# Seven block products in place of eight in the second inner layer of passes 13 to 15, with block sums on GpSimd

## The chip, the cores and the metric

One NeuronCore of one Trainium2 chip. The metric is the device time of one launch in microseconds (us). The kernel before takes 1303.97 us (median of three runs, 1303.16 to 1304.44).

## The reference, cut to what matters

For x of shape 4 x 1024 tokens x 256 features:

```python
x = x + 0.5 * ffn(layernorm(x))        # first feed-forward
x = x + attn(layernorm(x))             # a long convolution, gelu, 256 x 256 projection
x = x + 0.5 * ffn(layernorm(x))        # second feed-forward, same weights

def ffn(x):                            # einsum('bsi,oi->bso') * a scale per output
    h = silu(lin(x, w1, s1)) * lin(x, w2, s2)   # 256 -> 1024
    h = gelu(lin(h, h1, s_h1))                  # 1024 -> 1024, first inner layer
    h = gelu(lin(h, h2, s_h2))                  # 1024 -> 1024, second inner layer
    return lin(h, w3, s3)                       # 1024 -> 256
```

All weights of the feed-forward are -1, 0 or 1; the scales are float32. The result is float32.

## The kernel before, in words

**Passes.** The 4096 tokens are eight chunks of 512. A pass takes one chunk through one feed-forward, so there are 16 passes: 0 to 7 the first feed-forward, 8 to 15 the second. The convolution of batch b runs in eight units beside passes 4 to 13. Passes 13, 14 and 15 have almost only the feed-forward left; in the first slots of pass 13 the last batch is projected (`projection`, L1492) and added (`residual`, L889).

**Precision.** Each activation tile (128 features x 512 tokens) is kept as two float16 tiles, a high part and a low part, and every weight tile is multiplied by both into the same float32 sum in PSUM. The weights are exact in float16. One inner layer is 8 output tiles x 8 input tiles x 2 parts = 128 matmuls of 128 x 512.

**What each engine does in an inner layer.** For output tile s TensorE adds up its 16 products in a PSUM bank (`hidden`, L1413). ScalarE applies gelu in the bank (`gelu`, L1176) and makes the high part (`split_high`, L1166); VectorE makes the low part (`split_low`, L641) and with it a sum into `los`, from which the end of the program learns whether all numbers were finite. The next layer needs both parts of all eight tiles. So that TensorE need not wait for the last of them, it begins a layer with its first three output tiles side by side: their products with input tiles 0 to 5, then 6, then 7 (`EARLY`).

**Slots.** The order on every engine is written out in the program; nothing is chosen on the chip. A pass has 26 slots: 0 to 7 first inner layer, 8 to 15 second, 16 to 25 the mixed part, where TensorE makes the up projections of the next pass and the two down groups of this one. `T(i, s)` is slot s of pass i. In each slot an engine does its part of the layer and then what `fixed` (VectorE, L907) or `slot` (ScalarE, TensorE) puts there: for the next pass the statistics (`sums`, L676), from them the scales on GpSimd (`scales_of`, L1028), the normalised input (`norm`, L1186) and its low part (`norm_low`, L703). These stand in slots that `norm_slots` gives: in pass 13 `sums` and `scales_of` in slot 5, `norm` in 7 and 11, `norm_low` in 8 and 12; in pass 14 `sums` and `scales_of` in slot 2, `norm` in 4 and 7, `norm_low` in 5 and 8. In pass 15 there is no next pass.

**Queues are in order.** An instruction that waits holds up all that stands behind it on its engine. In `fixed`, `same` comes ahead of `sums`.

**PSUM.** Five banks (psf) go round for the feed-forward, three (pss) serve the convolution and the projection. Projection pairs 0 and 3 both use bank pss0, so pair 3 waits for the residual of pair 0.

**The check of the weights.** `same` (L710) compares a float16 weight piece with the float32 original, which SyncE loads again (`load_again`, L1604): 11 pieces of 2048 columns, in passes 13 to 15.

**The end.** Behind the last inner layer come the down products of pass 15 in three groups; VectorE multiplies and adds each (`down`, L661), checks the sums, and SyncE stores the rows.

## Time and profile before

| | |
|---|---|
| median of three runs | 1303.97 us |
| the profiled execution's own time | 1306.01 us |
| its span, first to last instruction | 1304.2 us |
| TensorE (PE) busy | 1293.1 us, 99% of the span |
| VectorE (DVE) busy | 888.8 us, 68% |
| ScalarE (ACT) busy | 762.9 us, 58% |
| GpSimd (POOL) busy | 402.6 us, 31% |
| mean granted TensorE clock | 0.999 of 2.4 GHz |

The profiled execution takes 1.81 us more than its span, and 2.04 us more than the median of the runs. A line such as "L1421 PE MATMUL psf<-hab,wall" is a group of instructions of one line of the program: engine, operation, destination and sources by their names. "x" is a count.

### The profile page before, as it was taken

Reading aid. Unit: us, or ns where it says so; the run is one execution under the profiler, and the core shown is the slowest. Engines: PE = TensorE matmul, PEld = TensorE weight load, DVE = VectorE, ACT = ScalarE, POOL = GpSimd, SP = SyncE. Lnnn points to the kernel's source line nnn. Section 1 sums busy time; section 2 is a strip of 40 time slices with the busy share of each in tenths; the row PEclk is TensorE's granted clock in tenths of the full one; section 3 lists DMA queues with packets and bytes.
Section 4 is the critical chain, followed back from the end, with each engine's and each line's share of the span. In section 5 each row is a group of like instructions: output and inputs, shape, how many; then the busy total and the mean of one; then the engine's idle time right before and its main releaser. Section 6 shows DMA issues by size and latency. Waiting matters only on the chain.

```text
span 1304.2 us, 17940 instructions
## 1 busy us (share of the span) xinstructions
PE 1293.1 (99%) x7039; PEld 653.2 (50%) x7039; DVE 888.8 (68%) x1768; ACT 762.9 (58%) x1245; POOL 402.6 (31%) x396
## 2 busy tenths in 40 slices
PE   9999999999999999999999999999999999999998
PEld 3454454644545445455454554545545455454544
DVE  5287768432546987988779887898877974454723
ACT  4664556845457467574775747757467564545433
POOL 6821377700012422633226333262332600001000
PEclk9999999999999999999999999999999999999999
DMA  8310000000010000000000000000000002221300
GB/s 314 136 41 9 9 1 17 1 9 9 1 53 13 2 15 1 17 1 1 17 1 17 9 9 17 17 12 14 9 17 17 9 17 74 81 81 56 138 1 19
DMA packets 45469, 41.80 MB, mean 32 GB/s; under 512 B 32704, under 2 KB 42432, under 8 KB 42688
## 3 DMA queue, kind: packets, MB, share of 16 engines
q1 hardware_dynamic: 45232, 40.56, 10.2%
q8 instruction: 57, 0.93, 0.3%
q14 instruction: 36, 0.29, 0.1%
q10 hardware_dynamic: 144, 0.02, 0.0%
HBM read 28.51 MB, written 4.19 MB: 25 GB/s over the span
## 4 chain that ended last, share of the span: by engine, by line
PE 93%; DVE 5%; issue 1%; ACT 1%; POOL 0%; POOLq 0%; DVEq 0%
PE psf L1421 66%; PE psf L1409 15%; PE psf L1433 7%; PE pss L1498 2%; DVE hab L645 1%; PE pss L1478 1%; DVE arena L602 1%; PE pss L1488 1%; PE pss L1449 1%; DVE xr L886 1%; DVE xr L674 0%; DVE psf L668 0%; DVE arena L605 0%; PE pss L1463 0%; DVE ht L657 0%
## 5 line engine op out<-in xcount | busy, mean ns | idle before, releaser
L1421 PE MATMUL psf<-hab,wall 128*128 128x512 f16 x4096 | 890.7, 379 | 2.8 <-DVE xr L674 1.8
L1421 PEld LDWEIGHTS psf<-hab,wall 128*128 128x128 f16 x4096 | 400.1, 98 | 482.4 <-DVE xr L674 3.2
L1180 ACT ACTIVATE psf<-psf,scf 128x512 f32<-128x512 f32 x256 | 168.7, 659 | 383.5 <-PE psf L1421 382.7
L645 DVE SCALAR_TENSOR_TENSOR hab<-psf,hab 128x512 f16<-128x512 f32 x256 | 174.9, 687 | 278.6 <-ACT hab L1173 277.7
L1409 PE MATMUL psf<-h,wall 128*128 128x512 f16 x1024 | 234.8, 381 | 1.0 <-ACT h L1184 0.7
L1173 ACT ACTIVATE hab<-psf 128x512 f16<-128x512 f32 x256 | 152.8, 597 | 8.1
L1409 PEld LDWEIGHTS psf<-h,wall 128*128 128x128 f16 x1024 | 99.8, 98 | 115.1 <-issue 2.5
L657 DVE SCALAR_TENSOR_TENSOR ht<-psf,scf,sil 128x512 f32<-128x512 f32 x128 | 93.9, 748 | 85.7 <-PE psf L1409 44.0
L1032 POOL TENSOR_SCALAR rs<-mv 128x4 f32<-128x4 f32 x16 | 5.3, 334 | 456.0 <-DVE mv L688 456.0
L1163 ACT ACTIVATE sil<-psf,scf 128x512 f32<-128x512 f32 x128 | 86.2, 685 | 83.0 <-PE psf L1409 82.2
L1433 PE MATMUL psf<-wall,hab 128*128 128x256 f16 x1024 | 117.1, 273 | 0.3
L1433 PEld LDWEIGHTS psf<-wall,hab 128*128 128x128 f16 x1024 | 99.3, 98 | 17.2 <-DVE xr L674 1.8
L645 DVE SCALAR_TENSOR_TENSOR hab<-ht,hab 128x512 f16<-128x512 f32 x128 | 105.8, 834 | 2.5
L834 DVE TENSOR_TENSOR arena<-arena,g 128x896 f32<-128x896 f32 (+6 forms) x112 | 103.4, 927 | 2.1
L1173 ACT ACTIVATE hab<-ht 128x512 f16<-128x512 f32 x128 | 80.2, 627 | 28.2 <-DVE ht L657 27.7
L837 DVE TENSOR_TENSOR arena<-arena 128x896 f32<-128x896 f32 (+6 forms) x112 | 96.2, 859 | 0.3
L1084 POOL TENSOR_TENSOR arena<-arena 128x1024 f32<-128x1024 f32 x8 | 23.2, 2895 | 235.8 <-ACT arena L1271 235.8
L1095 POOL TENSOR_TENSOR arena<-arena,g 128x896 f32<-128x896 f32 (+6 forms) x56 | 85.6, 1528 | 27.1 <-DVE hab L645 23.6
L1099 POOL TENSOR_TENSOR arena<-arena 128x896 f32<-128x896 f32 (+6 forms) x56 | 89.8, 1603 | 4.2
L1193 ACT ACTIVATE xnp<-xr,rn,rs 128x128 f32<-128x128 f32 x120 | 49.1, 481 | 3.5 <-POOL rn L1040 3.2
L1163 ACT ACT_TABLE_LOAD x31 | 39.8, 1283 | 0.5
L602 POOL TENSOR_TENSOR g16b<-arena 128x16 f32<-128x16 f32 (+5 forms) x72 | 35.7, 517 | 2.8
(143 smaller groups left out, 917.4 us busy)
## 6 DMA issues: line engine op xcount, KB each, us to landing
arena<-wh SPq DMA_DIRECT2D x8, 1024.0 KB, 5.4
g<-wh SPq DMA_DIRECT2D x6, 1024.0 KB, 9.2
out<-xr SPq DMA_DIRECT2D x15, 256.0 KB, 2.2
xr<-x SPq DMA_DIRECT2D x7, 512.0 KB, 5.0
arena<-w SPq DMA_DIRECT2D x3, 1024.0 KB, 5.1
g<-w SPq DMA_DIRECT2D x2, 1024.0 KB, 6.6
xr<-wh SPq DMA_DIRECT2D x2, 1024.0 KB, 9.5
g<-w SPq DMA_DIRECT2D x2, 512.0 KB, 6.0
```

Of the source, the lines that this page charges most:

```text
L645: e.scalar_tensor_tensor(out=hab[:, buffer(p), m, 1, :], in0=source(p), scalar=2.0 ** E2 if l else 1.0, in1=hab[:, buffer(p), m, 0, :], op ...
L657: e.scalar_tensor_tensor(out=source(p), in0=psf[bank_use(i, "up", 2 * m + 1) % MAIN][:, :], scalar=scf[:, 1, m:m + 1], in1=sil[:, m % 2, : ...
L834: muls[j] = ch.done(e.tensor_tensor(tv, xf[:, c, 0:NB - j], gj, ALU.mult))
L837: total = free[ti] = ch.done(e.tensor_tensor(acc[:, c, j:NB], acc[:, c, j:NB], tv, ALU.add))
L1095: k = ch.done(e.tensor_tensor(tv, xf[:, 0, 0:NB - j], g3[:, 0, j, ds].unsqueeze(1).to_broadcast([P, NB - j, P]), ALU.mult))
L1099: add = e.tensor_tensor(acc[:, 0, j:NB], acc[:, 0, j:NB], tv, ALU.add)
L1163: e.activation(sil[:, m % 2, :], psf[bank_use(i, "up", 2 * m) % MAIN][:, :], ACT.Silu, scale=scf[:, 0, m:m + 1]).then_inc(s_silu, 1)
L1173: e.activation(hab[:, buffer(p), m, 0, :], source(p), ACT.Copy, scale=2.0 ** E2 if l else 1.0).then_inc(s_hi, 1)
L1180: e.activation(bank, bank, ACT.Gelu, scale=scf[:, 2 + l, m:m + 1]).then_inc(s_gelu, 1)
L1409: ins = e.matmul(bank[:, :], W12[:, m // 4, l, k, ms], h0[:, k, part, :], start=(k == 0 and part == 0), stop=(k == 1 and part == 1))
L1421: ins = e.matmul(bank[:, :], WH[:, l, m // 2, k, ms], hab[:, buffer(p), k, part, :], start=(k == 0 and part == 0), stop=(k == KH - 1 and p ...
L1433: ins = e.matmul(bank[:, half:half + D], hab[:, buffer(p), k, part, P * t:P * (t + 1)], W3[:, k, :], start=(k == 0 and part == 0), stop=(k ...
```

## The change

The second inner layer of passes 13, 14 and 15 is computed as a 2 x 2 block product with seven block products. Weights are cut into four blocks of 512 x 512 (A11, A12, A21, A22), activations into four of 512 features x 256 tokens. For each of the seven products one weight block (or a sum of blocks) is multiplied with one activation block (or a sum of blocks), and the results are added to the four output blocks. A product is 4 output tiles x 4 input tiles x 2 parts = 32 matmuls of 128 x 256.

- **Sums of weight blocks.** Four (`sum_weights`), on VectorE, once: in slot 15 of pass 12 and in slots 0, 2 and 4 of pass 13. They are float16.
- **Sums of activation blocks.** The output tiles of the first inner layer come in the order 0, 4, 1, 5, 2, 6, 3, 7; two that follow each other are a quad q (tiles q and q+4, four blocks of 128 x 256). Gelu goes to SBUF (`gelu_words`). `turn_tokens` makes the sums T1 and T3 (one operation of 512 columns), T2 and T4 (256 each). GpSimd does it for quads 0, 1 and 2, in its slots 1, 3 and 4 and behind what stands there already; VectorE for quad 3. Then the high and low parts of seven blocks are made: for quads 0 to 2 one operation of 1792 columns on ScalarE (`high_quad`) and one on VectorE (`low_quad`), for quad 3 in parts of 768, 512 and 512 columns.
- **Products.** A PSUM tile holds two products, left and right half, and there are 14 tiles per layer. The first seven tiles take their left halves for input tiles 0, 1, 2 and then 3 side by side. All eight banks go round in passes 13 to 15 (`fast_uses`), each reused for the eighth use after it.
- **Output sums.** VectorE adds the halves (`first_sums`, `middle_sums`, `last_sums`: 512, 512 + 256 and 512 columns per quad), ScalarE copies one tile in two quads (`keep`), applies gelu in SBUF (twice 512) and makes the high parts, VectorE the low parts.
- **The last down products** of pass 15 take rows 0, 4, 1, 5, then 2, 6, then 3, 7, for three token tiles side by side ahead of the last two rows.
- **Checks.** `same` moves to other slots (T(13, 6), (13, 20), (13, 23), (14, 2), (14, 4), (14, 20), (14, 23), (15, 0), (15, 2), (15, 4), (15, 6)), works in place, and its pieces are loaded into xr rows once the output of these has been stored. `check_ternary` in pass 3 tests w*w*w = w for the second inner layer's weights: eight times two float16 products and one comparison of 1024 columns.

```diff
-SAME_AT = [T(13, s) for s in (9, 10, 14, 25)] + [T(14, s) for s in (2, 3, 10, 11, 12, 25)] + [T(15, 3)]
-
-AGAIN = {13: ((0, 1), (2, 3, 4, 5)), 14: ((), (6, 7, 8, 9, 10))}
+SAME_AT = [T(13, s) for s in (6, 20, 23)] + [T(14, s) for s in (2, 4, 20, 23)] + [T(15, s) for s in (0, 2, 4, 6)]
+AGAIN = {13: ((0, 1), (2, 3)), 14: ((4,), (5, 6, 7, 8)), 15: ((), (9, 10))}
+TERNARY = range(6, 10)
+CUBES_BESIDE = [2000] * 16 + [700] * 4 + [1400, 700, 700, 1400, 700, 700]
...
+FAST = 13
+QD, HF = KH // 2, CH // 2
+ROWS = [m + QD * r for m in range(QD) for r in range(2)]
+G12, G11, G22, G21, T1, T3, T2, T4 = range(8)
+U1, U3, U2 = T1, T3, T2
+WIDE = 7 * HF
+OPERAND = {1: G11, 2: G21, 3: G22, 4: T4, 5: T1, 6: T2, 7: T3}
+T_PARTS = ((G11, T1), (T1, T2), (T2, T4 + 1))
...
+SUMS_OF_WEIGHTS_AT = {T(12, 15): 0, T(13, 0): 1, T(13, 2): 2, T(13, 4): 3}
+def parts(l, q):
+    if l == 2:
+        return ((0, 2), (2, 4)) if q + 1 == QD else ((0, 4),)
+    return T_PARTS if q + 1 == QD else ((G11, T4 + 1),)
...
+def tiles_of(i):
+    return [t for q in (0, 2) for t in [("keep", i, q)] + [(kind, i, q + n) for n in range(2)
+                                                           for kind in ("first", "middle", "last")]]
...
+        def released(use):
+            kind, i, n = use
+            if kind == "h":
+                return s_gelu, gelus(i, n)
+            if kind == "u":
+                return (s_gate if n % 2 else s_silu), KH * i + n // 2 + 1
+            if kind == "d":
+                return s_xup, 2 * i + n + 1
+            n = quad(i, n) + 1
+            return {"keep": (s_kept, (n + 1) // 2), "first": (s_u1, n), "middle": (s_c22, n), "last": (s_c1221, n)}[kind]
...
+        def turned(i, q, n):
+            if q + 1 == QD:
+                return s_tokens, 3 * (i - FAST) + n
+            return s_tokensp, 3 * ((QD - 1) * (i - FAST) + q) + n
+        def turn_tokens(e, w, i, q):
+            g, sem = words[q % 2], turned(i, q, 0)[0]
+            w.wait_ge(s_gelu, gelus(i, 2 * q + 1))
+            e.tensor_tensor(both(at(g, T1, 2)), both(at(g, G11, 2)), spread2(at(g, G12)), ALU.subtract).then_inc(sem, 1)
+            w.wait_ge(*turned(i, q, 1))
+            e.tensor_tensor(at(g, T2), at(g, T3), at(g, G11), ALU.add).then_inc(sem, 1)
+            w.wait_ge(*turned(i, q, 2))
+            e.tensor_tensor(at(g, T4), at(g, G21), at(g, T2), ALU.subtract).then_inc(sem, 1)
...
+            def low_quad(i, l, q):
+                for n in range(len(parts(l, q))):
+                    k = split_of(i, l, q, n)
+                    high, low_, of = halves_to(i, l, q, n)
+                    w.wait_ge(s_hiq, k)
+                    c = N_FFN_SPLITS - N_QUAD_SPLITS + k - 1
+                    e.scalar_tensor_tensor(out=low_, in0=of, scalar=2.0 ** E2, in1=high, op0=ALU.mult, op1=ALU.subtract,
+                                           accum_out=los[:, c:c + 1]).then_inc(s_loq, 1)
...
+            def first_sums(i, q):
+                n, g = quad(i, q), words[q % 2]
+                w.wait_ge(s_tile["first"], n + 1)
+                w.wait_ge(s_kept, n // 2 + 1)
+                w.wait_ge(s_loq, words_free(i, 2, q))
+                e.tensor_tensor(two(g, G11, U1 - G11), both(fast_tile("first", i, q)[:, :]),
+                                spread2(at(kept[n // 2 % 2], n % 2)), ALU.add).then_inc(s_u1, 1)
+            def middle_sums(i, q):
+                n, g = quad(i, q), words[q % 2]
+                bank = fast_tile("middle", i, q)
+                w.wait_ge(s_tile["middle"], n + 1)
+                w.wait_ge(s_u1, n + 1)
+                e.tensor_tensor(both(at(g, U3, 2)), both(bank[:, :]), spread2(at(g, U1)), ALU.add).then_inc(s_u23, 1)
+                w.wait_ge(s_u23, n + 1)
+                e.tensor_tensor(at(g, G22), at(bank, 0), at(g, U2), ALU.add).then_inc(s_c22, 1)
+            def last_sums(i, q):
+                n, g = quad(i, q), words[q % 2]
+                w.wait_ge(s_tile["last"], n + 1)
+                w.wait_ge(s_u23, n + 1)
+                e.tensor_tensor(two(g, G12, G21 - G12), both(fast_tile("last", i, q)[:, :]), both(at(g, U3, 2)),
+                                ALU.add).then_inc(s_c1221, 1)
...
+            def sum_weights(which):
+                a11, a12, a21, a22 = (WH[:, 1, 2 * r:2 * r + 2, QD * c:QD * (c + 1), :] for r in range(2) for c in range(2))
+                s1, s2, s3, s4 = (t[:, :, :, :] for t in sums16)
+                if which == 0:
...
+            def fast_layers(i):
+                for s in range(KH):
+                    if s % 2:
+                        if s == 7:
+                            turn_tokens(e, w, i, 3)
+                        low_quad(i, 1, s // 2)
+                    slot(i, s)
+                slot(i, 8)
+                slot(i, 9)
+                first_sums(i, 0)
+                middle_sums(i, 0)
+                slot(i, 10)
+                last_sums(i, 0)
+                slot(i, 11)
+                first_sums(i, 1)
+                middle_sums(i, 1)
+                last_sums(i, 1)
+                slot(i, 12)
+                low_quad(i, 2, 0)
+                first_sums(i, 2)
+                middle_sums(i, 2)
+                slot(i, 13)
...
+                if t in SUMS_OF_WEIGHTS_AT:
+                    time += sum_weights(SUMS_OF_WEIGHTS_AT[t])
...
+                    if i >= FAST and s in (1, 3, 4):
+                        turn_tokens(e, w, i, (1, 3, 4).index(s))
...
+            def keep(i, q):
+                n = quad(i, q) // 2
+                w.wait_ge(s_tile["keep"], n + 1)
+                if n > 1:
+                    w.wait_ge(s_u1, 2 * n - 2)
+                e.activation(kept[n % 2], fast_tile("keep", i, q)[:, :], ACT.Copy).then_inc(s_kept, 1)
+            def gelu_quad(i, q):
+                n, g = quad(i, q), words[q % 2]
+                upper, lower = (scf[:, 3, r:r + 1] for r in (q, q + QD))
+                w.wait_ge(s_u1, n + 1)
+                w.wait_ge(s_c1221, n + 1)
+                e.activation(at(g, G12, 2), at(g, G12, 2), ACT.Gelu, scale=upper).then_inc(s_gup, 1)
+                w.wait_ge(s_c22, n + 1)
+                e.activation(at(g, G22, 2), at(g, G22, 2), ACT.Gelu, scale=lower).then_inc(s_glow, 1)
+            def high_quad(i, l, q):
+                for n, (lo, hi) in enumerate(parts(l, q)):
+                    high, _, of = halves_to(i, l, q, n)
+                    if l == 1:
+                        w.wait_ge(s_gelu, gelus(i, 2 * q + 1))
+                        if hi > T1:
+                            w.wait_ge(*turned(i, q, 1 if hi <= T2 else 3))
+                    else:
+                        w.wait_ge(s_gup, quad(i, q) + 1)
+                        w.wait_ge(s_glow, quad(i, q) + 1)
+                    e.activation(high, of, ACT.Copy, scale=2.0 ** E2).then_inc(s_hiq, 1)
...
+            def fast_layers(i):
+                for s in range(KH):
+                    gelu_words(i, s)
+                    if s % 2:
+                        high_quad(i, 1, s // 2)
+                    slot(i, s)
+                slot(i, 8)
+                slot(i, 9)
+                keep(i, 0)
+                slot(i, 10)
+                gelu_quad(i, 0)
+                slot(i, 11)
+                gelu_quad(i, 1)
+                high_quad(i, 2, 0)
+                slot(i, 12)
+                keep(i, 2)
+                high_quad(i, 2, 1)
+                slot(i, 13)
+                gelu_quad(i, 2)
+                high_quad(i, 2, 2)
+                slot(i, 14)
+                slot(i, 15)
+                gelu_quad(i, 3)
...
+            def product(i, q, p, out, ks):
+                g = OPERAND[p]
+                ms = slice(P * (q % 2), P * (q % 2 + 1))
+                if p in (3, 5, 6, 7):
+                    w.wait_ge(s_wsum, 4)
+                for k in ks:
+                    w.wait_ge(s_loq, split_of(i, 1, k, PART_OF[g] if len(parts(1, k)) == 3 else None))
+                    if p in (1, 2, 4):
+                        stationary = WH[:, 1, q // 2 + 2 * (p == 4), k + QD * (p != 1), ms]
+                    else:
+                        stationary = sums16[{5: 0, 6: 1, 7: 2, 3: 3}[p]][:, q // 2, k, ms]
+                    for part in range(2):
+                        a = WIDE * part + HF * (g - G11)
+                        ins = e.matmul(out, stationary, regions[k][:, a:a + HF], start=(k == 0 and part == 0),
+                                       stop=(k + 1 == QD and part == 1))
+                return ins
...
+                tiles = tiles_of(i)
+                early, banks = tiles[:7], []
+                for k in range(QD - 1):
+                    for n, use in enumerate(early):
+                        if not k:
+                            banks.append(fast_bank(*use))
+                        left(use, banks[n], (k,))
+                    slot(i, KH + k)
+                for kinds in (("keep", "first", "last"), ("middle",)):
+                    for n, use in enumerate(early):
+                        if use[0] in kinds:
+                            left(use, banks[n], (QD - 1,))
+                for n, use in enumerate(tiles):
+                    if n >= len(early):
+                        banks.append(fast_bank(*use))
+                        left(use, banks[n], range(QD))
+                    right(use, banks[n])
...
-            for t in (0, 2):
-                down(i, t, banks[t // 2], 0, range(KH - 1), False)
+            banks = [fast_bank("d", i, g) for g in range(len(groups(i)))]
+            for rows in (ROWS[:4], ROWS[4:6]):
+                for t in (0, 2, 3):
+                    fast_down(i, t, banks[max(t - 1, 0)], 0, rows, False)
             for g, (t0, n) in enumerate(groups(i)):
                 for t in range(t0, t0 + n):
-                    down(i, t, banks[g], D * (t - t0), (KH - 1,) if t % 2 == 0 else range(KH), t + 1 == t0 + n)
+                    fast_down(i, t, banks[g], D * (t - t0), ROWS if t == 1 else ROWS[6:], t + 1 == t0 + n)
...
-                    w.wait_ge(s_dve, mark["ylo", 2 * B - 1][1])
+                    for c in range(4):
+                        w.wait_ge(s_out[c], 16 * len(groups(NC + c)))
```

## Rows read from the trace of the kernel before

**Rows 1.** The page's first part: busy us, share and instructions of each engine.
```profile
PE 1293.1 (99%) x7039; PEld 653.2 (50%) x7039; DVE 888.8 (68%) x1768; ACT 762.9 (58%) x1245; POOL 402.6 (31%) x396
```

**Rows 2.** Timeline of TensorE, passes 12 to 15: start, length, what, count.
```profile
1061.90 0.86 PE L1488 MATMUL pss<-cs,arena 128*128 128x64 f16 x24
...
1078.92 9.66 PE L1421 MATMUL psf<-hab,wall 128*128 128x512 f16 x44
...
1096.67 0.49 PE L1498 MATMUL pss<-wts,arena 128*128 128x256 f16 x3
...
1160.22 55.42 PE L1421 MATMUL psf<-hab,wall 128*128 128x512 f16 x256
1215.47 7.07 PE L1409 MATMUL psf<-h,wall 128*128 128x512 f16 x32
1222.38 3.66 PE L1433 MATMUL psf<-wall,hab 128*128 128x256 f16 x32
1225.87 3.62 PE L1409 MATMUL psf<-h,wall 128*128 128x512 f16 x16
...
1291.53 5.19 PE L1433 MATMUL psf<-wall,hab 128*128 128x256 f16 x46
```

**Rows 3.** Groups by shape, GpSimd: busy, mean ns of one, idle before.
```profile
L1037 POOL TENSOR_TENSOR rs<-rs,half 128x4 f32<-128x4 f32 x16 | 21.0, 1314 | 1.3
...
L602 POOL TENSOR_TENSOR g16b<-arena 128x512 f32<-128x512 f32 x12 | 13.9, 1179 | 0.5
...
L1099 POOL TENSOR_TENSOR arena<-arena 128x512 f32<-128x512 f32 x8 | 11.3, 1413 | 0.4
...
L602 POOL TENSOR_TENSOR g16b<-arena 128x256 f32<-128x256 f32 x12 | 7.3, 633 | 0.5
```

**Rows 4.** Groups by shape, ScalarE.
```profile
L1180 ACT ACTIVATE psf<-psf,scf 128x512 f32<-128x512 f32 x256 | 168.7, 659 | 383.5 <-PE psf L1421 382.7
...
L1156 ACT ACTIVATE wall<-g 128x2048 f16<-128x2048 f32 x5 | 9.5, 1901 | 0.0
```

**Rows 5.** Groups by shape, VectorE.
```profile
L645 DVE SCALAR_TENSOR_TENSOR hab<-psf,hab 128x512 f16<-128x512 f32 x256 | 174.9, 687 | 278.6 <-ACT hab L1173 277.7
...
L716 DVE SCALAR_TENSOR_TENSOR arena<-arena,wall 128x2048 f16<-128x2048 f32 x11 | 25.2, 2290 | 6.2 <-DMA arena<-wh 6.2
...
L724 DVE SCALAR_TENSOR_TENSOR arena<-arena 128x1024 f16<-128x1024 f32 x16 | 18.9, 1220 | 0.0
```

**Rows 6.** Timeline of VectorE, pass 14: the end of the statistics for pass 15.
```profile
1177.87 0.38 DVE L688 BATCH_NORM_AGGREGATE mv<-st 128x2 f32<-128x6 f32 x4
```

**Rows 7.** Timeline of GpSimd, pass 14: the last two of four scale operations.
```profile
1178.89 3.01 POOL L1037 TENSOR_TENSOR rs<-rs,half 128x4 f32<-128x4 f32 x1
1181.98 0.20 POOL L1040 TENSOR_TENSOR rn<-rn,rs 128x4 f32<-128x4 f32 x1
```

**Rows 8.** Timeline of ScalarE, pass 14: one half of the next pass's input.
```profile
1182.22 1.65 ACT L1193 ACTIVATE xnp<-xr,rn,rs 128x128 f32<-128x128 f32 x4 [3.24 <-POOL rn L1040]
1183.90 0.63 ACT L1197 ACTIVATE xnp<-xnp 128x512 f16<-128x512 f32 x1
```

**Rows 9.** Timeline of VectorE around slot 15 of pass 12.
```profile
1060.01 1.22 DVE L724 SCALAR_TENSOR_TENSOR arena<-arena 128x1024 f16<-128x1024 f32 x1
1061.16 0.08 DVE L724 DVE_READ_ACCUMULATOR arena<-arena 128x1 f32 x1
```

**Rows 10.** Timeline of VectorE, the last down groups, first and last of six.
```profile
1296.75 0.70 DVE L668 TENSOR_TENSOR psf<-psf,s3b 128x512 f32<-128x512 f32 x1 [1.05 <-PE psf L1433]
...
1299.41 0.42 DVE L674 TENSOR_TENSOR xr<-xr,psf 128x256 f32<-128x256 f32 x1
```

**Rows 11.** Stretches of 2 us near the start: busy times, then granted clock (PEclk), DMA.
```profile
8.00:10.00 2.00, 1.33 (x8) 0.62 (x7) 1.59 (x7) 1.31 (x3) 1.24 (x3) 1.00 1.06 435
10.00:12.00 2.00, 1.66 (x5) 0.54 (x5) 0.93 (x2) 0.06 (x2) 0.56 (x2) 0.59 1.01 426
12.00:14.00 2.00, 2.00 (x7) 0.71 (x6) 0.40 (x1) 0.64 (x1) 1.69 (x1) 0.56 1.02 430
```

More of the change, by code:

```diff
@@ L1 @@
+import itertools
 import math
@@ new lines, in halves_to @@
+        def halves_to(i, l, q, part):
+            lo, hi = parts(l, q)[part]
+            if l == 1:
+                a, z = HF * (lo - G11), HF * (hi - G11)
+                return regions[q][:, a:z], regions[q][:, WIDE + a:WIDE + z], at(words[q % 2], lo, hi - lo)
+            if hi - lo == 2:
+                row = q + QD * (lo // 2)
+                return hab[:, i % 2, row, 0, :], hab[:, i % 2, row, 1, :], at(words[q % 2], lo, 2)
+            tiles = hab[:, i % 2, q:q + QD + 1:QD, :, :]
+            return tiles[:, :, 0, :], tiles[:, :, 1, :], both(at(words[q % 2], 0, 4))
@@ L963, in slot @@
                 beside = TAPS_BESIDE if i < FIRST - 1 else PAIRED if paired else BESIDE
-                quota = (0 if s < 0 else beside[s]) - fixed(i, s)
-                strand.run(now["slot"], quota)
+                time = fixed(i, s)
+                strand.run(now["slot"], (0 if s < 0 else beside[s]) - time)
+                cubed.run(now["slot"], CUBES_BESIDE[s] - time)
             e.memset(one[:, :], 1.0).then_inc(s_init, 1)
@@ L1349, in act_program @@
             for i in range(PASSES):
-                for s in range(2 * KH):
-                    gelu(i, s)
-                    split_high(tile(i, 1, s))
-                    slot(i, s)
+                if i >= FAST:
+                    fast_layers(i)
+                else:
+                    for s in range(2 * KH):
+                        gelu(i, s)
+                        split_high(tile(i, 1, s))
+                        slot(i, s)
                 if i + 1 < PASSES:
-                    behind = tile(i + 1, 0, 0)
+                    behind = 0
                     for n, (what, m) in enumerate(MIXED):
@@ L1424, in hidden, with first_hidden @@
                         ins.then_inc(s_hid, 1)
+            def first_hidden(i, s, bank, ks):
+                row = ROWS[s]
+                ms = slice(P * (row % 2), P * (row % 2 + 1))
+                for k in ks:
+                    w.wait_ge(s_lo, tile(i, 0, k) + 1)
+                    for part in range(2):
+                        ins = e.matmul(bank[:, :], WH[:, 0, row // 2, k, ms], hab[:, i % 2, k, part, :],
+                                       start=(k == 0 and part == 0), stop=(k == KH - 1 and part == 1))
+                    if k == KH - 1:
+                        ins.then_inc(s_hid, 1)
@@ new lines, in fast_down @@
+            def fast_down(i, t, bank, half, rows, count):
+                for m in rows:
+                    q, r = m % QD, m // QD
+                    w.wait_ge(s_loq, split_of(i, 2, q, r if q + 1 == QD else None))
+                    for part in range(2):
+                        ins = e.matmul(bank[:, half:half + D], hab[:, i % 2, m, part, P * t:P * (t + 1)], W3[:, m, :],
+                                       start=(m == ROWS[0] and part == 0), stop=(m == ROWS[-1] and part == 1))
+                    if m == ROWS[-1] and count:
+                        ins.then_inc(s_down, 1)
```

234 lines of the change are left out of this document (205 added, 29 removed).

## The prediction

> **What bounds the kernel now.** The page's busy shares come first: TensorE is busy for 99% of the span, VectorE 68%, ScalarE 58% [rows 1]. Then its timeline over the last passes: one piece of work stands directly behind the other, 256 matmuls of both inner layers from 1160.22 to 1215.47 with no gap [rows 2]. So TensorE's instruction stream is the time, and a change pays what it takes out of the stream and costs each place at which TensorE now has to wait. The other engines must be followed in order, since before they always arrive early and after the change they have a longer way to go.
>
> **What goes.** A 512-column matmul takes (1215.47 - 1160.22)/256 = 0.2158 us, a 256-column one with a new weight tile each time (1225.87 - 1222.38)/32 = 0.1091 us [rows 2]. Before: 128 x 0.2158 = 27.63 us a layer. After: 7 x 32 x 0.1091 = 24.43 us. Gain 3.20 us, three times: **-9.6 us** (between -9 and -10).
>
> **Durations for what comes.** GpSimd's float32 sum of 512 columns took 1.18 us where it had little beside it and 1.41 in the convolution, 256 columns 0.63 [rows 3]: `turn_tokens` is 1.18 + 0.63 + 0.63 and two waits on itself of 0.1, at least 2.65; with 1.41 and the small ones longer in proportion 3.1. I take 2.75, nearer to the quiet row since VectorE mostly waits meanwhile. ScalarE: 0.66 for 512 columns, 1.90 for 2048 [rows 4], so 1.69 for 1792 and 0.87 for 768. VectorE: 0.69, 1.22 and 2.29 for 512, 1024 and 2048 columns [rows 5], so 2.0 for 1792 and 0.95 for 768; `turn_tokens` on VectorE 0.69 + 0.42 + 0.42 [rows 5, 10] and waits on itself, 1.65. A semaphore from one engine to the next costs some 0.05, from TensorE 0.2.
>
> **Pass 14, the large one.** Time 0 is the start of its first inner layer. Tiles are done at 9.5, 9.9, 10.4 (three side by side: 44 matmuls to the first), then 13.8, 17.3, 20.7, 24.2 and 27.6.
> - Quad 0: gelus end 11.05, GpSimd 13.85, ScalarE's high parts 15.6, VectorE's low parts 17.6.
> - Slot 2 of VectorE stands behind these low parts: `same` 2.25, ends 19.85, and only then `sums`, 1.8, ends 21.7. Before, `sums` ended at 1178.25 - 1160.22 = 18.0 [rows 2, 6].
> - GpSimd's slot 2 is `scales_of`, and it waits for these sums; quad 1 stands behind it in slot 3, though its gelus end at 17.0. Before, the last of the scale operations ended 3.93 us behind the sums [rows 6, 7]; the long one of them took 3.01 of that against a mean of 1.31 [rows 3], so I take 2.2: 23.9 (up to 25.6). Quad 1 on GpSimd: 26.65.
> - ScalarE has waited for it with quad 1's high parts: 28.4. Behind: gelu 4 29.1, `norm` 1.65 + 0.63 [rows 8] 31.35, gelu 5 32.05. Quad 2: GpSimd 34.9, ScalarE high 36.65, gelu 6 37.35, gelu 7 38.0; VectorE low parts of quad 2 38.65, `norm_low` 39.3, `turn_tokens` of quad 3 40.95, the first low part of quad 3 **41.95**.
> - TensorE would want quad 3 after 42 matmuls of the new layer, at 27.63 + 4.58 = 32.2. On its way there it also needs the banks of tiles 4, 5 and 6, which gelus 4, 5 and 6 free: it waits until 37.4 for the last, has 3.3 us of work, and then waits for quad 3. **+9.75 us** (9.0 to 12.5: the slow scales, +1.7, GpSimd at 1.41, +0.9).
>
> **Pass 13.** (Times of the trace.) `scales_of` is in slot 5, behind the three quads. But VectorE's low parts of quad 0 now stand ahead of residual 0. Tile 1 is done at 1090.2 and gelu at 1091.05; GpSimd 1093.85, ScalarE 1095.6, VectorE 1097.6, residual 0 1098.3. Projection 3, at 1096.67 before [rows 2], needs its bank: **+1.7** (1.4 to 2.2). Then tile 5 at 1106.6, quad 2's low parts at 1114.0 by the same chain (gelu, 2.75, 1.69, 2.0), behind them `sums` 1.8, `same` 2.25, `turn_tokens` 1.65, low part 0.95: 1120.75. TensorE is there at 1113.5 + 4.6 = 1118.1: **+2.65** (2.2 to 3.5).
>
> **Pass 15.** No scales and no norms. Time 0 as above: quad 1 on GpSimd 20.0, ScalarE 21.7, gelus 4 and 5 23.1, quad 2 on GpSimd 26.1, high 27.8, low 29.8, `same` in slot 6 32.1, `turn_tokens` 33.75, low part 34.7, against 32.2: **+2.5** (2.0 to 3.2).
>
> **Weight sums.** The first (2048 columns, float16) stands in slot 15 of pass 12 ahead of `y_low`, whose end at 1061.24 [rows 9] the inverse transform waits for, on TensorE at 1061.90 [rows 2]: cover 0.65. No row shows a float16 sum of two SBUF tensors. At the rate of the nearest row it is 2.29 [rows 5] and the wait 1.65; at twice that rate 1.15 and **+0.5**. I take 0.5, because float16 outputs are packed here and the other three sums are hidden either way (VectorE idles in slots 0, 2 and 4 ahead of each wait). The Trainium skill (VectorE: DVE Perf Modes, Mode 2x_1P) says that a two-tensor operation on packed 16-bit data gives two results a cycle; by it the term is 0.5, by the float32 row 1.65, and no row of before decides it. `check_ternary` is 24 operations, about 21 us, in pass 3, in portions of 2.6 us a slot beside a split of 0.7 in 3.45 us: 0.
>
> **Second layers and mixed parts.** From the first part of quad 3 on TensorE has 182 matmuls, 19.9 us. VectorE has 3.8 us per quad in it, ScalarE 2.3 and a copy; the last quad's high parts come behind the silu table load and silu 0, its low parts about 8.2 us after the layer, TensorE's first down row 3 at 8.2: 0 (to 0.3). `same` in slots 20 and 23 leaves VectorE 6 us behind the start of the next layer, which wants its last tile 9 us in: 0.
>
> **The end.** Before, 46 matmuls after the layer group 0 is done. After, 56 are (three tiles took their first six rows): +1.1; the last low part comes 4.4 us after the layer, TensorE wants row 7 at 4.15: +0.25. The VectorE chain behind, 1296.75 to 1299.83 [rows 10], stays. **+1.35** (1.1 to 1.8).
>
> **The clock.** In the first 10 us TensorE had short waits (1.33 of 2 us busy) and in the next 4 us its granted clock was 0.59 and 0.56, near 1.2 GHz [rows 11]: some 1.7 us lost. In pass 14 it works 0.9 us in the 9 us before 37.4. I expect the same fall there; 1.25 of what it costs lies in front of the wait for quad 3 anyway. **+1.0** (0 to 3.5). The Trainium skill (TensorE: Matmul & The Clock Gate, Part 1) has the two levels as a gate that follows TensorE's activity; by it the fall comes, and the waits of 1.7 to 2.7 us in passes 13 and 15 could bring it too.
>
> **Sum.** -9.6 + 9.75 + 1.7 + 2.65 + 2.5 + 0.5 + 1.35 + 1.0 = +9.85. Span 1304.2 + 9.8 = 1314.0, own time of the profiled execution 1315.8. That execution lies 2.04 above the median of the runs, so the median becomes 1303.97 + 9.8 = **1313.8 us**.
>
> **Rivals.**
> - *The waits are covered (faster).* One mechanism: the low parts of quad 3 are there when TensorE has done its 42 matmuls. It decides from 32.2 us after the first layer's start. Then 9.75, 2.65, 2.5 and the clock go and the sum is -6.0: 1297.9. For it: before, the layer's own work leaves VectorE and ScalarE 2 to 3 us idle in each slot. Against: the order of GpSimd's queue in pass 14, by which the chain reaches 41.95 with every duration at its lowest still beyond 41. If only pass 14 is covered, -0.9: 1303.1, no change. 7% and 6%.
> - *The clock falls widely (slower still).* It is low for 4 us behind each of the three waits: 1.7 us each, and in pass 14 with none absorbed: +5 in place of +1, 1317.8. For it: rows 11. Against: outside pass 14 no wait is longer than 2.7 us. 15%.
> - *Float16 sums and GpSimd at their slow rows.* +1.15, +0.9 and the slow scales +1.7: 1317.5. 9%.
> - *The 256-column products don't run at 0.1091.* If a product costs an eighth more than that, a layer takes 27.6 us again and the gain of 9.6 is gone: 1323.4. Against: 1024 matmuls of this shape at the steady rate. 3%.
> - The forecast as it stands: 60%.
>
> **How the numbers follow.** Its own range is 1310.5 to 1317; with the two slow rivals to 1318, and below to 1307.5 for parts of the chain that are shorter than I read them. What a measurement can tell from no change is 0.2%, 2.6 us. Faster 0.07, same 0.06, slower 0.87.
>
> **What would show it.** In the profile after: 224 matmuls a layer at 0.109; TensorE's longest waits in pass 14, for ScalarE's gelus and then for a VectorE low part, 9 to 10 us in all; GpSimd's first sum of quad 1 of pass 14 behind its scales; in pass 13 a wait of projection 3 for L889's successor. Wrong would be a GpSimd chain of quad 1 that starts at its gelus, or no wait above 3 us in pass 14.

## The result and the profile after

The changed kernel takes **1321.58 us** (median of 4 runs, 1320.70 to 1324.66) against 1303.97 before: ratio 1.0138, 95% interval 1.0125 to 1.0150. Slower was forecast, by 9.8 us; it became 17.6, outside the range. The profiled execution took 1320.70 us, span 1318.9, and its page begins:

```profile
PE 1285.7 (97%) x7327; PEld 681.4 (52%) x7327; DVE 954.3 (72%) x1831; ACT 771.5 (58%) x1236; POOL 436.0 (33%) x423
```

TensorE's share has fallen from 99% to 97% [rows 1]: its work shrank by 7.4 us, the span grew by 14.7. So the time lies in waits (and in matmuls that a slow clock stretched, which count as busy). Its timeline shows where, beside the place in which before stood 256 matmuls without a gap [rows 2] (start, length, what, count, and in brackets the idle time and what ended it; passes 3, 13, 14 and 15):

```profile
288.16 1.50 PE L1925 MATMUL pss<-g,arena 128*128 128x128 f16 x24 [1.38 <-ACT xr L794]
...
314.58 1.14 PE L1939 MATMUL pss<-arena,cs 128*128 128x256 f16 x9 [0.75 <-issue]
...
1079.74 9.66 PE L1817 MATMUL psf<-hab,wall 128*128 128x512 f16 x44
...
1099.34 0.50 PE L1974 MATMUL pss<-wts,arena 128*128 128x256 f16 x3 [1.69 <-DVE xr L1175]
...
1121.88 0.61 PE L1836 MATMUL pss<-arena,wall 128*128 128x256 f16 x4 [2.67 <-DVE arena L831]
...
1162.56 10.52 PE L1817 MATMUL pss<-hab,wall 128*128 128x512 f16 x48
...
1191.45 0.39 PE L1836 MATMUL psf<-arena,wall 128*128 128x256 f16 x2 [0.22 <-ACT arena L1487]
1194.22 0.39 PE L1836 MATMUL psf<-arena,g 128*128 128x256 f16 x2 [2.38 <-ACT arena L1487]
1200.23 0.61 PE L1836 MATMUL psf<-arena,g 128*128 128x256 f16 x2 [5.61 <-ACT g L1487]
...
1224.76 1.89 PE L1793 MATMUL psf<-h,wall 128*128 128x512 f16 x8
...
1245.56 10.52 PE L1817 MATMUL pss<-hab,wall 128*128 128x512 f16 x48
...
1278.89 0.61 PE L1836 MATMUL psf<-arena,g 128*128 128x256 f16 x2 [4.23 <-ACT g L1487]
...
1285.00 0.61 PE L1836 MATMUL pss<-arena,wall 128*128 128x256 f16 x4 [1.35 <-DVE arena L831]
...
1304.88 1.91 PE L1897 MATMUL psf<-wall,hab 128*128 128x256 f16 x16
```

From these starts and those of [rows 2] (before's pass 15 began at 1236.27) the difference comes apart, against the prediction's terms (us; a pass counts from its first inner layer to the next pass's, pass 15 to the end of its second layer):

| stretch | predicted | measured |
|---|---|---|
| pass 3 (`check_ternary`) | 0 | +2.44 |
| from there to pass 13 (drift; first weight sum) | +0.5 | +0.49 |
| pass 13: -3.2 + 1.7 + 2.65 | +1.15 | +1.52 |
| pass 14: -3.2 + 9.75 + clock 1.0 | +7.55 | +6.95 |
| pass 15: -3.2 + 2.5 | -0.7 | **+4.06** |
| the end | +1.35 | +1.35 |
| sum | +9.85 | +16.81 |

The start behind a wait moves by some 0.16 us more than its bracket says: without a wait, the next start lies that much ahead of a row's recorded end.

The two profiles are only 14.70 apart, because that of before had lost 2.11 at its start (its clock of [rows 11]; the profile after shows 1.00 there) and at 215 us. By about as much, 2.04, that execution lay above the median of its runs. The median after lies 0.88 above its own profiled execution: 16.81 + 0.88 = 17.7, against 17.6 between the medians.

### The profile page after: what moved, and what is told of

Read it like the earlier page. It is cut to its first block and busy times, and to the rows that moved or that the text cites. A ratio compares the mean times of both kernels' runs of the same rounds, so it can differ in the third digit from the quotient of the medians.

```text
span 1318.9 us, 18667 instructions
## 1 busy us (share of the span) xinstructions
PE 1285.7 (97%) x7327; PEld 681.4 (52%) x7327; DVE 954.3 (72%) x1831; ACT 771.5 (58%) x1236; POOL 436.0 (33%) x423
## 5 line engine op out<-in xcount | busy, mean ns | idle before, releaser
L1805 PE MATMUL psf<-hab,wall 128*128 128x512 f16 x3328 | 723.8, 379 | 2.1 <-DVE xr L957 1.7
L1805 PEld LDWEIGHTS psf<-hab,wall 128*128 128x128 f16 x3328 | 325.0, 98 | 392.0 <-DVE xr L957 3.2
L1474 ACT ACTIVATE psf<-psf,scf 128x512 f32<-128x512 f32 x208 | 136.9, 658 | 291.6 <-PE psf L1805 290.8
L810 DVE SCALAR_TENSOR_TENSOR hab<-psf,hab 128x512 f16<-128x512 f32 x208 | 141.8, 685 | 166.4 <-ACT hab L1467 165.5
L1793 PE MATMUL psf<-h,wall 128*128 128x512 f16 x976 | 223.2, 379 | 1.0 <-ACT h L1548 0.7
L1467 ACT ACTIVATE hab<-psf 128x512 f16<-128x512 f32 x208 | 124.2, 597 | 6.6
L820 DVE SCALAR_TENSOR_TENSOR hab<-ht,hab 128x512 f16<-128x512 f32 x120 | 98.8, 832 | 2.2
L1909 PE MATMUL psf<-wall,hab 128*128 128x256 f16 x832 | 95.1, 273 | 0.3
L1909 PEld LDWEIGHTS psf<-wall,hab 128*128 128x128 f16 x832 | 80.6, 98 | 13.9 <-DVE xr L957 1.8
L642 POOL TENSOR_TENSOR arena<-arena 128x512 f32<-128x512 f32 x6 | 9.2, 1539 | 178.4 <-ACT arena L1487 178.4
L1817 PE MATMUL psf<-hab,wall 128*128 128x512 f16 x288 | 63.3, 379 | 0.0
```

Source lines behind the costliest of these rows:

```text
L810: e.scalar_tensor_tensor(out=hab[:, buffer(p), m, 1, :], in0=source(p), scalar=2.0 ** E2 if l else 1.0, in1=hab[:, buffer(p), m, 0, :], op ...
L820: e.scalar_tensor_tensor(out=hab[:, i % 2, m, 1, :], in0=ht[:, n % 3, :], scalar=1.0, in1=hab[:, i % 2, m, 0, :], op0=ALU.mult, op1=ALU.su ...
L1467: e.activation(hab[:, buffer(p), m, 0, :], source(p), ACT.Copy, scale=2.0 ** E2 if l else 1.0).then_inc(s_hi, 1)
L1474: e.activation(bank, bank, ACT.Gelu, scale=scf[:, 2 + l, m:m + 1]).then_inc(s_gelu, 1)
L1793: ins = e.matmul(bank[:, :], W12[:, m // 4, l, k, ms], h0[:, k, part, :], start=(k == 0 and part == 0), stop=(k == 1 and part == 1))
L1805: ins = e.matmul(bank[:, :], WH[:, l, m // 2, k, ms], hab[:, buffer(p), k, part, :], start=(k == 0 and part == 0), stop=(k == KH - 1 and p ...
```

## The experiments

**e1, the scale operations behind the three quads of pass 14 too.**

```
-    if i == FIRST - 1 or i > FIRST and (i - FIRST) % 2 == 0:
+    if i == FIRST - 1 or i > FIRST and (i - FIRST) % 2 == 0 or i == 14:
```

> The changed kernel, with the statistics, scales, norms and their low parts of pass 14 in the slots that pass 13 uses (5, 7 and 11, 8 and 12), so that GpSimd's scales stand behind the three quads. Theory (order of GpSimd's queue, and VectorE beside it): quad 1 of pass 14 then starts at its gelus, but now beside VectorE's comparison in slot 2, and quad 2 beside the one in slot 4, so that GpSimd takes some 5.3 us a quad as in pass 15 and not 2.75. Pass 14, from the start of its first inner layer to the end of its second, goes from 62.2 us to about 59, the whole to about 1318.4. Rival (the order alone, GpSimd's sums always 2.75): the wait of 8.2 us goes down to 1.5 and the slow clock with it, 54 us for the pass, about 1313.5 for the whole.

Measured: 1319.12 us (1317.83 to 1320.86), ratio 1.0117 [1.0100, 1.0134]. Both layers of pass 14 took 58.8 us in place of 62.2: TensorE waited 4.24 and 0.69 there. As expected (59 us, 1318.4), the wait for the scales is gone and a new one stands in its place, of the size that pass 15 has. GpSimd in this pass:

```profile
1174.17 1.26 POOL L642 TENSOR_TENSOR arena<-arena 128x512 f32<-128x512 f32 x1 [51.72 <-ACT arena L1487]
1175.51 0.72 POOL L644 TENSOR_TENSOR arena<-arena 128x256 f32<-128x256 f32 x1
1176.31 0.72 POOL L646 TENSOR_TENSOR arena<-arena 128x256 f32<-128x256 f32 x1
1180.06 1.95 POOL L642 TENSOR_TENSOR g<-g 128x512 f32<-128x512 f32 x1 [3.02 <-ACT g L1487]
1182.09 2.65 POOL L644 TENSOR_TENSOR g<-g 128x256 f32<-128x256 f32 x1
1184.82 0.72 POOL L646 TENSOR_TENSOR g<-g 128x256 f32<-128x256 f32 x1
```

Quad 0 has the quiet durations, 2.7 us in all, which the forecast took for every quad. Quad 1 takes 5.3, and one of its two small sums 2.65 in place of 0.72.

**e2, no comparison in the slots of the first inner layer of pass 15** (a third buffer takes piece 9).

```
-... + [T(15, s) for s in (0, 2, 4, 6)]
+... + [T(15, 0)] * 3 + [T(15, 8)]
```

> The changed kernel, with the comparisons of weight pieces 7, 8 and 9 all in slot 0 of pass 15 and that of piece 10 in slot 8 (piece 9 is loaded into a third buffer), so that none of them runs beside GpSimd's block sums in pass 15. Theory (VectorE's comparison slows GpSimd): the 256-column sums of quads 1 and 2 take 0.72 us and not 2.65, TensorE's waits of 4.2 and 1.35 us in pass 15 go, with them the slow clock; both inner layers of pass 15 take 54.5 us in place of 59.3, the whole -4.8, about 1316.8. Rival (GpSimd is slow in pass 15 for a reason of its own, or the comparison in slot 6 was what counted): the sums stay at 2.65, and only the 2.3 us of the comparison in slot 6 go.

Measured: 1317.49 us (1317.15 to 1318.21), ratio 1.0099 [1.0082, 1.0116]. Pass 15 took 53.4 us in place of 59.3, its waits were 0.54 and 0.44, and the small sums were all back at 0.72. Two things went: 1.93 us on GpSimd for each of quads 1 and 2, and on VectorE the comparison of slot 6, 2.2, which stood ahead of quad 3's sums and which the forecast had counted. This run doesn't tell the two apart; g3 below has the first alone. Of these 5.9 us the median shows 4.1: behind the same waits the rest of pass 13 took 21.55 us in this profile and 19.88 in the changed kernel's, and pass 14 was 1.5 us longer (on this see e3 and f1).

**e3, all block sums on VectorE.**

```
-                        if s == 7:
-                            turn_tokens(e, w, i, 3)
+                        turn_tokens(e, w, i, s // 2)
...
-                    if i >= FAST and s in (1, 3, 4):
-                        turn_tokens(e, w, i, (1, 3, 4).index(s))
```

> The changed kernel, with VectorE making the block sums of all four quads (ahead of its low parts, in slots 1, 3, 5 and 7) and GpSimd none. Theory: each sum chain takes 1.65 us in place of 2.75 to 5.3 and doesn't stand behind the scales, but stands behind VectorE's comparisons. By the chains: projection 3 waits 0.6 in place of 1.7, pass 13 for quad 3 1.5 in place of 2.7; pass 14 56.6 us from first layer's start to second's end in place of 62.2, pass 15 56.4 in place of 59.3; in all -10.8, about 1310.8. Rival (VectorE becomes the bound, its order with 5 us more in each pass): the waits of passes 14 and 15 stay at 5 us or more, within 3 us of the changed kernel.

Measured: 1313.46 us (1312.09 to 1313.78), ratio 1.0066 [1.0049, 1.0083]. The waits: projection 0.38, pass 13 quad 3 2.31, pass 14 2.81, pass 15 1.11 and 2.66. That is 2.7 above the 1310.8 expected: pass 14 came as foreseen (56.7 us), pass 15 took 57.9 for 56.4, and pass 13 gained nothing (82.83 us to the next pass's start, 82.82 in the changed kernel), though its waits were 1.7 us shorter. Behind the 2.31 the clock fell (stretches of 2 us; the number behind POOL's is the granted clock):

```profile
1117.00:1119.00 2.00, 0.95 (x9) 0.60 (x7) 1.93 (x5) 0.56 (x1) 1.84 (x3) 1.00 0.00 0
1119.00:1121.00 2.00, 0.74 (x6) 0.66 (x7) 2.00 (x6) 1.41 (x4) 1.18 (x2) 0.95 0.00 0
1121.00:1123.00 2.00, 2.00 (x12) 1.40 (x10) 0.80 (x3) 1.57 (x4) 0.00 (x0) 0.50 0.00 0
1123.00:1125.00 2.00, 2.00 (x15) 1.57 (x14) 0.32 (x1) 0.46 (x1) 0.00 (x0) 0.70 0.23 47
```

The 182 matmuls from there on took 21.55 us against 19.88 in the changed kernel. In this order of the queues GpSimd's sums cost 8.1 us more than VectorE's; what still lies above the kernel before is queueing on VectorE, as f3 shows.

**e4, residual 0 of pass 13 one slot earlier**, ahead of quad 0's low parts.

```
+                at_residual = (0, 2, 3, 4) if i == FAST else RESIDUAL_AT
```

> The changed kernel, with the residual of projection pair 0 in slot 0 of pass 13, ahead of VectorE's low parts of quad 0, in place of slot 1. Theory: the wait of projection 3 (1.69 us) goes and nothing takes its place, since the chain of quads 1 to 3 starts from TensorE's tiles: -1.7, about 1319.9. Rival: TensorE only comes earlier to its next wait, for quad 3 (2.67 us, becomes 4.4): no change.

Measured: 1323.13 us (1322.97 to 1323.49), ratio 1.0144 [1.0127, 1.0161]. Projection 3 waited no more, but quad 3 waited 4.36 in place of 2.67, so the second wait had taken over the whole gain. GpSimd's first sum of quad 2 began 1.9 us earlier and ended at the same moment; below it the VectorE operation beside it:

```profile
1106.65 3.39 POOL L642 TENSOR_TENSOR arena<-arena 128x512 f32<-128x512 f32 x1 [4.40 <-ACT arena L1488]
```

```profile
1106.63 2.28 DVE L878 SCALAR_TENSOR_TENSOR g<-wall 128x2048 f16<-128x2048 f16 x1
```

VectorE's ends at 1108.91 and GpSimd's at 1110.04, 1.13 behind it, nearly the quiet duration of 1.26. That fits not a slower sum but a sum that has not begun.

**f1 and g2, the check of pass 3 from slot 6 on** (`yield At(T(3, 0))` becomes `yield At(T(3, 6))`), and **g1, the changed kernel once more** beside g2.

> The changed kernel with one edit: the cubes that stand for four comparisons in pass 3 begin at slot 6 of that pass in place of slot 0, behind the statistics of the next pass on VectorE's queue. Theory (the two waits of TensorE in pass 3, 1.38 us at 288.16 and 0.75 us at 314.58, are VectorE's statistics and low halves standing behind the cubes): the 1.38 goes for certain, and the second only as far as fewer cubes are queued ahead of the low halves of the taps; the time falls by 1.4 to 2.4 us, to about 1319.5. Rival (the cubes only have to be worked off later, and the low halves of the taps at slot 11 then stand behind more of them): the second wait grows, and the time stays within 0.5 us of 1321.6 or rises.

> The changed kernel as it is, in more rounds, beside g2 on one chip, because the median of the version with the later check did not move although 1.50 us of pass 3 were gone from its profile. Theory (the 1.66 us by which the second inner layer of pass 13 was longer in that profile, 21.54 in place of 19.88 us, come from the granted clock falling after the wait of 2.67 us, and that falls on some executions of either kernel): the two medians differ by the 1.5 us of pass 3 once enough executions are there, this one at about 1321.6 to 1322 and g2 at about 1320.3. Rival (the later check costs elsewhere what it gives in pass 3): no difference between the two.

> The version with the check of pass 3 from slot 6, again. Theory: 1.2 to 1.8 us below g1. Rival: within 0.5 us of it.

Measured: f1 1321.61 us (1320.97 to 1324.21), ratio 1.0141 [1.0125, 1.0156]; g2 1322.24 (1321.97 to 1322.45), 1.0138 [1.0121, 1.0155]; g1 1322.24 (1321.54 to 1323.84), 1.0141 [1.0124, 1.0159]. The profiles show the gain: the wait of 1.38 is gone, that at slot 11 stays (0.87), and all that follows is 1.50 earlier. The times don't. In both profiles of the later check the 182 matmuls of pass 13 took 21.54 us behind the same wait of 2.67, in g2 at a granted clock of 0.68 and 0.76 in two stretches of 3 us from 1120; in both of the changed kernel 19.88, in g1 at 1.00. The gain of 1.50 was given back there (1.66). So my theory on the median fell, and its rival (no difference) came true. Why the clock falls at one starting time and not at another 1.5 us later stays open.

**f2, everything apart, GpSimd's sums; f3, the same with VectorE's sums.** Beside e2's and f1's edits and e4's residual: no comparison at all between slots 1 and 7, weight sums 1 to 3 all in slot 0 of pass 13, and the statistics for the next pass between quad 2's sums and its low parts:

```
+SAME_AT = [T(13, s) for s in (8, 20, 23)] + [T(14, s) for s in (0, 8, 20, 23)] + [T(15, 0)] * 3 + [T(15, 8)]
+SUMS_OF_WEIGHTS_AT = {T(12, 15): (0,), T(13, 0): (1, 2, 3)}
+    if i >= FAST:
+        return 5, (7, 11), (8, 12)
...
+                        if s == 5 and i + 1 < PASSES:
+                            sums(i + 1)
                         low_quad(i, 1, s // 2)
```

> The changed kernel with every long VectorE operation taken out of the slots in which GpSimd makes block sums: the float16 sums of the weight blocks all ahead of pass 13's first layer, the comparisons at the pass's ends (three at T(15,0), one of them into a third buffer) and ahead of the second layer, the first residual one slot earlier, the statistics of passes 14 and 15 behind quad 2's turn in slot 5, and the check of pass 3 from slot 6 on. GpSimd keeps the block sums of quads 0 to 2. Theory (the sums themselves cost 2.7 us on a quiet GpSimd, and only what stands beside them made them slow): passes 14 and 15 take 53 to 54 us each from the first layer to the end of the second, as the pass did that had its comparisons apart (53.4), pass 3 gives back up to 2.4, and the time is about 1303 to 1306, level with the kernel before. Rival (GpSimd's sums are too slow in themselves: the turn of a quad through GpSimd is longer than TensorE's work on a quad): waits of over 1.5 us stay in each pass and the time is above 1309.

> As the last one, and VectorE makes the block sums of all four quads, 1.53 us each in the records of the run that had them there. Theory (seven products save 3.2 us of TensorE in each of three passes, and all that stood against it was queueing on VectorE and GpSimd): passes 13 to 15 take 52 to 53 us from the first layer to the end of the second, where before they took 55.2; pass 3 gives back up to 2.4 us; from the 1313.5 of the version with the sums on VectorE alone go 2.3 + 1.7 in pass 13, 4.1 in pass 14, 5.2 in pass 15 and 1.4 to 2.4 in pass 3, which makes 1297 to 1300: faster than the kernel before by 5 to 8 us. Rival (VectorE is full in these passes, so that what leaves one slot is late in another): it stays above 1303.

Measured: f2 **1299.55 us** (1299.37 to 1300.19), ratio 0.9966 [0.9952, 0.9979]; f3 **1296.94 us** (1296.87 to 1297.67), ratio 0.9946 [0.9933, 0.9960]: 0.3% and 0.5% below the kernel before, small but clear of the noise. f3's TensorE has no wait left in the three passes:

```profile
1229.26 10.52 PE L1819 MATMUL pss<-hab,wall 128*128 128x512 f16 x48
...
1256.89 0.60 PE L1838 MATMUL pss<-arena,wall 128*128 128x256 f16 x4
...
1281.34 1.91 PE L1899 MATMUL psf<-wall,hab 128*128 128x256 f16 x16
```

27.63 us for the first layer and 24.45 for the second, as the prediction had them (27.63 and 24.43). f2 waited 0.39 and 0.44 in each of passes 14 and 15 and not at all in pass 13, and its granted clock stayed at 1.00 behind these waits. It went 3.5 us below the expected 1303 to 1306.

**g3 and g4, one comparison put back** into slot 2 of pass 15 (`[T(15, 0)] * 3` becomes slots 0, 0, 2), in f2 and in f3.

> The version with everything apart and GpSimd's sums (1299.55 us), and one comparison of 128x2048 words put back into slot 2 of pass 15, beside GpSimd's sums of quad 1; VectorE is idle there for 4.5 us, from 1248.1 to 1252.6. Theory (the two engines slow each other): the sums of quad 1 take 5.3 us in place of 3.4, all that follows the quad is 2 us later, TensorE's wait at quad 1, 0.39 us, becomes about 2.4, and the time is 1301.5 to 1303. Rival (only queueing counts): the comparison lies in idle time of its own engine and costs nothing, 1299.6.

> The version with everything apart and VectorE's sums (1296.94 us), with the same one comparison put back into slot 2 of pass 15. Here the sums of quad 1 stand behind it on VectorE's queue: 2.2 us later for certain, from which the quad has about 1.7 us in hand (its high half begins 18.5 us after the first layer, and with GpSimd's sums a start at 20.6 made TensorE wait 0.39 us). Theory and rival alike: 0.3 to 0.8 us more, 1297.2 to 1297.8. The difference between this and the last version's increment is the price of the two engines' meeting.

Measured: g3 1301.71 us (1301.11 to 1305.12), ratio 0.9985 [0.9975, 0.9994], 2.2 above f2; g4 1297.05 (1296.78 to 1297.36), ratio 0.9946 [0.9929, 0.9962], level with f3: there the 2.2 us of queueing fitted into the slack, which was larger than I had read it. In g3, GpSimd and then VectorE:

```profile
1247.42 1.95 POOL L644 TENSOR_TENSOR g<-g 128x512 f32<-128x512 f32 x1 [3.02 <-ACT g L1494]
1249.45 2.65 POOL L646 TENSOR_TENSOR g<-g 128x256 f32<-128x256 f32 x1
1252.18 0.72 POOL L648 TENSOR_TENSOR g<-g 128x256 f32<-128x256 f32 x1
```

```profile
1246.22 2.03 DVE L833 SCALAR_TENSOR_TENSOR arena<-arena 128x1792 f16<-128x1792 f32 x1 [7.63 <-ACT arena L1526]
...
1248.18 3.35 DVE L1003 SCALAR_TENSOR_TENSOR xr<-xr,wall 128x2048 f32<-128x2048 f32 x1
```

Read the ends in turn. The low parts end at 1248.2, and GpSimd's first sum, recorded from 1247.42, ends 1.1 later, at 1249.4; the comparison, recorded from 1248.18, ends 2.2 behind that, at 1251.5; GpSimd's second sum ends 0.6 behind that, at 1252.1. Each works only when the other has ended. TensorE's wait at the quad grew from 0.39 to 2.31. Behind it the granted clock fell in the profiled execution (0.50 from 1263 to 1265), which took 1302.55 us; the ten runs lie 1.6 to 5.6 above f2's median.

**h1, in the same place a VectorE operation with one source**, a sum over 2048 words that nobody uses.

```
+                if t == T(15, 2):
+                    w.wait_ge(s_same, 10)
+                    e.reduce_sum(spare[:, :], again[1], AXX)
```

> The version with everything apart and GpSimd's sums (1299.55 us), and in slot 2 of pass 15, where g3 had a comparison of two tensors, an additional sum over 2048 float32 words of one tensor whose result nobody uses: about as long on VectorE (2.2 us), but with one source in SBUF in place of two. Theory (an operation with two sources in SBUF and GpSimd's sums exclude each other: each waits until the other has ended, which fits 1.95, 2.65 and 3.34 us; one with a single source leaves GpSimd alone): the small sums of quad 1 stay at 0.72 us, TensorE's waits at 0.39 and 0.44, the time at 1299.3 to 1299.9. Rival (any long VectorE operation slows GpSimd, by bandwidth or by the sequencers): the sums take 1.5 us and more in place of 0.72, and the time is 1301 or above.

Measured: 1299.91 us (1299.38 to 1301.43), ratio 0.9971 [0.9958, 0.9983], level with f2. GpSimd, then VectorE:

```profile
1247.67 1.96 POOL L645 TENSOR_TENSOR g<-g 128x512 f32<-128x512 f32 x1 [3.02 <-ACT g L1498]
1249.70 0.73 POOL L647 TENSOR_TENSOR g<-g 128x256 f32<-128x256 f32 x1
```

```profile
1248.42 2.28 DVE L1203 TENSOR_REDUCE spare<-xr 128x1 f32<-128x2048 f32 x1
```

It ran through both sums, and neither was longer than in f2 (1.95, behind the low parts, and 0.72). TensorE's waits in pass 15 were 0.55 and 0.44, where 0.39 and 0.44 were expected: quad 0's first sum had taken 1.40 us beside the end of the slot 0 comparisons. So a long VectorE operation alone doesn't hold GpSimd up.

One difference is left: the reduction writes one column, the comparison 2048. The kernel before settles it. There GpSimd makes pairs of sums (L602) beside `split_low` (L645). This always writes 512 float16 columns to SBUF, and its second source `hab` lies in SBUF; its first is `ht` in SBUF or `psf` in PSUM. GpSimd, then VectorE:

```profile
163.96 2.96 POOL L602 TENSOR_TENSOR g16b<-arena 128x512 f32<-128x512 f32 x2
...
240.22 2.05 POOL L602 TENSOR_TENSOR g16b<-arena 128x512 f32<-128x512 f32 x2
```

```profile
165.16 0.86 DVE L645 SCALAR_TENSOR_TENSOR hab<-ht,hab 128x512 f16<-128x512 f32 x1
...
165.95 1.52 DVE L645 SCALAR_TENSOR_TENSOR hab<-ht,hab 128x512 f16<-128x512 f32 x1
...
241.27 0.69 DVE L645 SCALAR_TENSOR_TENSOR hab<-psf,hab 128x512 f16<-128x512 f32 x1 [1.57 <-ACT hab L1173]
```

With both sources in SBUF the pair of sums takes 2.96 us and VectorE's operation up to 1.52; with one in PSUM 2.05 and 0.69, though the two overlap. So the second source in SBUF decides, not the length of the operation and not its output.

## Why the prediction was wrong

The direction was right, and so were pass 13, pass 14 and the end. Missing were 7.8 us: 4.8 in pass 15, 2.4 in pass 3 and the 0.9 by which the median lies above the profiled execution, less 0.2 in the other rows of the table.

**Pass 15, "+2.5 (2.0 to 3.2)": the step that failed, 4.8 us.** It was built on "I take 2.75, nearer to the quiet row since VectorE mostly waits meanwhile". In slots 2 and 4 VectorE doesn't wait, the comparison stands there, as the prediction itself lists for slot 2 of pass 14. The changed kernel's pass 15, GpSimd and the comparison:

```profile
1262.49 1.95 POOL L642 TENSOR_TENSOR g<-g 128x512 f32<-128x512 f32 x1 [3.02 <-ACT g L1487]
1264.52 2.65 POOL L644 TENSOR_TENSOR g<-g 128x256 f32<-128x256 f32 x1
1267.24 0.73 POOL L646 TENSOR_TENSOR g<-g 128x256 f32<-128x256 f32 x1
1270.99 1.95 POOL L642 TENSOR_TENSOR arena<-arena 128x512 f32<-128x512 f32 x1 [3.02 <-ACT arena L1487]
1273.02 2.65 POOL L644 TENSOR_TENSOR arena<-arena 128x256 f32<-128x256 f32 x1
```

```profile
1263.24 3.34 DVE L998 SCALAR_TENSOR_TENSOR xr<-xr,wall 128x2048 f32<-128x2048 f32 x1
```

Two quads took 5.3 us each in place of 2.75. Against the forecast's stations quad 1 left GpSimd 2.4 us late (22.4 behind the layer's start for 20.0) and quad 2 4.8 late (30.9 for 26.1), and from there every step had nearly its forecast length. The first low part of quad 3, below, ended at 39.4 for 34.7, and TensorE went on at 39.44 (1285.00). That is the whole miss:

```profile
1283.98 0.95 DVE L831 SCALAR_TENSOR_TENSOR arena<-g,arena 128x768 f16<-128x768 f32 x1
```

The rows of the forecast were no bounds, because the collision was already in them. The 1.18 taken as quiet is the mean of L602: seven of its twelve sums took 1.05, and the two beside `hab<-ht,hab`, shown above, 1.50. e2, g3, g4 and h1 show the cause from four sides. The Trainium skill (SBUF — State Buffer, Who interferes with whom) has this rule: a VectorE instruction with two SBUF inputs and a GpSimd one that reads SBUF contend for a shared pair of ports, which is locked and not divided. The Trainium skill (GPSIMD Engine Reference, 1. Specifications) names the same contention. The trace agrees to 0.15 us: behind the other's end come 1.12, 2.16 and 0.57 us in g3, for quiet durations of 1.26, 2.29 and 0.72. The forecast should have weighed it; the rows above make it 2.6 us more for each of quads 1 and 2, 0.7 behind the low parts and 1.9 behind the comparison.

**`check_ternary`, "0": 2.44 us.** This term too failed by its mechanism. Its length, 21 us, and the portions were right, and VectorE has room in pass 3. But the portion stands ahead of the statistics for the next pass on VectorE's queue: they ended at 280.98, 1.9 later than before, against a TensorE that was 2.1 earlier. ScalarE's normalisation waited for them through GpSimd's scales, and behind it the copy that TensorE's next tap products need (L794): a wait of 1.38, starts 1.55 later. The low halves of the taps came 1.5 later: a wait of 0.75, starts 0.9 later. f1 took the first away. The room of an engine says nothing on the order of its queue.

**The clock, "+1.0": size, 0.2 in the profiled execution.** In pass 14 of the profiled execution it was 0.57, 0.50, 0.50 and 0.72 in the four stretches of 2 us from 1196 on. It cost only some 0.2 us: TensorE reached quad 3 at 1204.89, and quad 3's first low part ended at 1204.65, so that most of the loss took the place of the third wait. In g1's profile, the same kernel, the clock stayed at 0.50 until 1204, TensorE reached quad 3 at 1206.08, and the pass took 84.21 us in place of 83.00; such executions can be the 0.9 of the median (the other runs lie 0.5 to 4 us above the profiled one, with mean clocks of 0.992 to 0.994 in place of 0.995, but no trace of them shows the place). In pass 15 the clock fell as well (0.55 and 0.60 in the 4 us from 1278) and cost nothing, since TensorE then waited 1.35 for quad 3 anyway. The forecast had such a fall only in a rival (*the clock falls widely*, 15%).

**Right.** The products: 0.1092 us each. Projection 3: 1.69 for 1.7. Quad 3 of pass 13: 2.67 for 2.65. Pass 14: statistics for pass 15 ended at 1184.27, 21.7 us behind the layer's start as worked out; TensorE's last wait for a bank ended 37.67 behind it for 37.4; both layers 62.2 us for 62.8. There GpSimd had quiet durations for quad 1 (1.27, 0.72, 0.72; for quad 2 the first sum took 1.96), because quad 1 stood behind the scales and so behind the comparison: the same delay that made pass 14 slow kept the two engines apart, and e1, which took it away, let them meet. The first weight sum took 1.22 us for 2048 float16 columns, near half of the 2.29 of [rows 5], and TensorE waited 0.36 for what stood behind it (0.5 forecast). The end: +1.35. The rival of covered waits, -6.0, is what f3 became, 6.6 below the kernel before in its own batch (1303.58), by VectorE's queue put in another order and with all block sums on it, not by slack that was there.
